# Twelve-stage decoder: latent attention's projections made pair by pair in two banks, and two expert mixtures reordered

## The chip, the cores and the metric

One core of a Trainium2 chip runs the whole program. The engines are TensorE (PE, with its weight loads PEld), VectorE (DVE), ScalarE (ACT), GpSimd (POOL) and SyncE (SP), which issues DMAs here. The metric is the device time of one execution in microseconds, median of the runs; lower is better.

## The reference

A decoder of four layers, each with an attention, a cross attention and a feed-forward part; after each of the twelve, x = layernorm(x + part(x)). x is 8 batches of 256 tokens, 256 wide, all in float32. The change touches four of the twelve parts:

```
_L0_xattn, _L1_xattn (latent attention, 16 heads of 64, context of 77 rows a batch):
    xn = layernorm(context); latn = layernorm(x); q = latn @ Wq
    k, v = split(concat([xn, latn]) @ Wkv)          # 77 + 256 = 333 keys
    out = softmax(q k' / 8) v @ Wo
_L0_ffn (mixture with silu, 8 experts, 2 chosen):
    probs = softmax(x @ router_w); topw, topi = top_k(probs, 2)
    routed = sum over the chosen e: topw * (silu(x @ w1[e]) @ w2[e])
    shared = sigmoid(x @ shared_gate_w) * ((silu(gate) * up) @ shared_down),  gate, up = x @ shared_gate_up
_L1_ffn (mixture with relu, 16 experts of 64, 4 chosen):
    sum over the chosen e: sel_val * (relu(x @ keys[e]) @ values[e])
```

## The kernel before

The twelve parts are twelve stages, `build[k](k)`, each with a program for every engine. Within one the engines meet at semaphores, each engine runs its instructions strictly in the written order, and nothing of one stage runs beside the next. x lives in SBUF by token (`x_nat`) and transposed (`x_t`). Two arenas of weights take turns: a stage's pack lies in one, the next pack is loaded into the other. PSUM is eight banks: `S.R` (2 x 2), `S.T` (2), `S.O` (2).

**Latent attention, `perceiver`** (stages 1 and 4). A prologue makes what batch 0 needs: `FIRST` lists its jobs. `lat` transposes the normalised latents, `q0` to `q3` project queries (four heads each), `c0` to `c4` transpose the contexts (only in the first such stage), `w0` to `w9` make the context values of all batches, which go to DRAM and come back by batch, `k0` to `k7` project the keys of one pair of heads each, `v0` to `v3` the values of half the heads for one block of keys. Then the loop over 8 batches of 8 pairs of heads. A pair on TensorE is: scores of both halves of the queries, the product of the pair before with its values, job slot 0, transposes of the first half, slot 1, transposes of the second half, slot 2. VectorE takes the maxima, copies the product, divides, and copies half of the transposes; ScalarE takes exponentials and copies the other half. `PERCEIVER_JOBS` names the jobs of the 24 slots of a batch: in the kernel before those of the next batch, but `o0`, `o1` (output projection) and `tail` (transposes of the new x), which belong to the batch before, and `v3`. All use one bank, `S_x`, so a job waits until the one before is copied out (`x_done`, counted over both copying engines). VectorE copies k and o, ScalarE all others.

**Silu mixture, `moe_silu`** (stage 2). TensorE makes the router's logits; VectorE ranks the choices and lays out 39 tiles of 128 rows, each with one expert. The shared expert runs for batches 0 to 4 beside that (`EARLY`), with the products and adds on POOL, for 5 to 7 behind the tiles. The tile loop: POOL issues an indirect gather (8 ahead, `XB`), TensorE transposes the rows, multiplies, transposes, multiplies, with copies on ScalarE and VectorE; POOL issues an indirect scatter into `planes` in DRAM, one plane for first and one for second choices. In the end both planes are read back by SP in four quarters, and x + weight 1 * plane 0 + weight 2 * plane 1 is built by VectorE, ScalarE (`weighed`) and POOL (`joined`), then normalised and transposed.

**Relu mixture, `moe_relu`** (stage 5). Four hidden units of two 128-wide blocks each for every batch; VectorE takes relu and gate in one step (`clipped`) out of PSUM; `outputs` multiplies by the values. The set-up of the gates is a VectorE chain; TensorE runs the hidden units of batch 0 and fillers (`keep_warm`, matmuls whose result nobody reads) beside it.

## Time and profile before

| | us |
|---|---|
| median of 3 runs | 3190.68 |
| lowest and highest run | 3190.6 and 3209.84 |
| the profiled execution's own time | 3193.03 |
| its span, first to last instruction | 3191.2 |
| TensorE busy in the span | 2893.4 (91%) |
| VectorE, ScalarE, POOL busy | 1909.2 (60%), 1192.7 (37%), 344.1 (11%) |
| mean granted TensorE clock | 0.97 |

Busy time of TensorE is modelled for the ends of matmuls. The stages that are touched lie at 376.8 to 978 (first perceiver), 978 to 1174 (silu mixture), 1336.8 to 1936.8 (second perceiver) and 1936.8 to 2090.9 (relu mixture). Names of tiles in the rows: `arena` is a pack of weights or a buffer in the spare arena, so `arena`, `v`, `k_t`, `q_t` alternate by batch.

### The profile page before, as it was taken

How to read it: one execution, taken by the hardware profiler on the slowest of the kernel's cores; microseconds unless marked ns; L12 is line 12 of the kernel's file. 1: busy time of each engine (PE TensorE's matmuls, PEld its weight loads, DVE VectorE, ACT ScalarE, POOL GpSimd, SP SyncE). 2: the span in 40 equal slices, each digit the busy share in tenths (PEclk: the TensorE clock that was granted, in tenths of full speed). 3: DMA queues.
4: the chain of work that ended last, by engine and by line, in shares of the span. 5: the costliest groups of instructions: out<-in, count | busy, mean ns of one | idle time of the engine just before them, and what ended most of it. 6: DMA issues, size and time to landing. Idle time of an engine off the chain costs nothing. (4 is left out here: it accounts for less than half of the span.)

```text
span 3191.2 us, 54962 instructions
## 1 busy us (share of the span) xinstructions
PE 2893.4 (91%) x22402; PEld 1838.4 (58%) x22402; DVE 1909.2 (60%) x3405; ACT 1192.7 (37%) x2549; POOL 344.1 (11%) x474
## 2 busy tenths in 40 slices
PE   6999899999988968799999989989999899989898
PEld 3565556666656746556666656856655433336576
DVE  4666347766774344447766773325547899985532
ACT  1332234444442333234444441123323476643111
POOL 1111100000003720000000000000011100000222
PEclk9999999999999979899999999989999999999899
DMA  3001010000011331010000000010000100000242
...
DMA packets 43419, 103.90 MB, mean 33 GB/s; under 512 B 4962, under 2 KB 32848, under 8 KB 39586
## 3 DMA queue, kind: packets, MB, share of 16 engines
...
## 5 line engine op out<-in xcount | busy, mean ns | idle before, releaser
L2360 ACT ACTIVATE prob<-R,neg_max 128x333 f32<-128x333 f32 x512 | 268.4, 537 | 209.1 <-DVE neg_max L2427 209.1
L3910 DVE TENSOR_TENSOR_SCAN arena<-arena,u 128x512 f32<-128x512 f32 x256 | 289.4, 1197 | 0.1
L2249 PE MATMUL T<-const,prob 128*128 128x128 f32 (+1 forms) x1536 | 211.4, 274 | 36.5 <-DVE prob L2440 23.4
L2249 PEld LDWEIGHTS T<-const,prob 128*128 128x128 f32 (+1 forms) x1536 | 181.2, 143 | 106.3 <-DVE prob L2440 68.6
L2440 DVE TENSOR_TENSOR prob<-prob,rec 128x666 f32<-128x666 f32 x256 | 218.3, 853 | 20.1 <-issue 1.3
L2427 DVE TENSOR_REDUCE neg_max<-R 128x2 f32<-128x666 f32 x256 | 205.3, 843 | 36.7 <-PE R L2238 36.7
L2367 ACT ACTIVATE prob_t<-T 128x384 f32<-128x384 f32 x256 | 125.5, 490 | 245.6 <-PE T L2249 239.3
L2433 DVE COPY prob_t<-T 128x384 f32<-128x384 f32 x256 | 141.9, 554 | 95.9 <-PE T L2249 80.8
L3841 ACT ACTIVATE arena<-delta,neg_a 128x510 f32<-128x510 f32 x256 | 176.0, 714 | 45.2 <-DVE arena L3910 44.3
L2186 PE MATMUL O<-keys_in,arena 128*128 128x333 f32 x512 | 174.6, 466 | 4.7 <-ACT attn_t L2342 1.4
L3744 PE MATMUL R<-arena,diag 64*64 64x512 f32 x1024 | 135.1, 616 | 26.5 <-DVE arena L3910 26.4
L2191 PE MATMUL O<-arena,keys_in 128*128 128x512 f32 x256 | 126.4, 617 | 2.6 <-ACT arena L2339 1.4
L2182 PE MATMUL O<-keys_in,arena 128*128 128x256 f32 x512 | 125.7, 389 | 2.4 <-ACT keys_in L2333 2.4
L2186 PEld LDWEIGHTS O<-keys_in,arena 128*128 128x128 f32 x512 | 87.9, 189 | 55.4 <-DVE arena L2408 5.4
L2209 PE MATMUL O<-arena,attn_t 128*128 128x256 f32 x512 | 118.9, 385 | 1.0 <-DVE ysb L2410 1.0
L944 DVE TENSOR_REDUCE neg_max<-R 128x8 f32<-128x2048 f32 (+1 forms) x24 | 55.0, 2291 | 100.0 <-PE R L721 100.0
L2209 PEld LDWEIGHTS O<-arena,attn_t 128*128 128x128 f32 x512 | 94.8, 190 | 25.2 <-issue 11.8
L2182 PEld LDWEIGHTS O<-keys_in,arena 128*128 128x128 f32 x512 | 92.1, 189 | 26.5 <-issue 10.8
L2360 ACT ACTIVATION_READ_ACCUMULATOR prob<-R,neg_max 128x1 f32 x512 | 103.9, 203 | 0.0
L2266 PE MATMUL O<-prob_t,v 128*64 128x256 f32 (+1 forms) x768 | 97.2, 388 | 1.3 <-DVE prob_t L2433 1.3
L2408 DVE COPY arena<-O 128x333 f32<-128x333 f32 x64 | 32.3, 504 | 109.1 <-PE O L2186 109.1
L2266 PE MATMUL O<-prob_t,arena 128*64 128x256 f32 (+1 forms) x768 | 97.2, 388 | 0.0
...
## 6 DMA issues: line engine op xcount, KB each, us to landing
...
```

The costliest lines, as they stand in the source:

```text
L2182: last = nc.tensor.matmul(bank[:, h * T:(h + 1) * T], wq[:, c, (2 * i + h) * P:(2 * i + h + 1) * P], keys[:, c, CTX:XK], start=(c == 0), s ...
L2186: last = nc.tensor.matmul(bank[:, 0:XK], wkv[:, c, i * P:(i + 1) * P], keys[:, c, :], start=(c == 0), stop=(c == C - 1))
L2209: last = nc.tensor.matmul(bank[:, 0:D], attn_t[:, b % 2, c, i * P:(i + 1) * P], wo[:, c, :], start=(c == 0), stop=(c == HP - 1))
L2249: last = nc.tensor.transpose(S.T[0:n, i, kc * P:(kc + 1) * P], prob[:, g % 2, i, first:first + n], S.ident)
L2266: last = nc.tensor.matmul(S_o[XD * i:XD * (i + 1), 0:T], v[b % 2][0:n, kc, (2 * hp + i) * XD:(2 * hp + i + 1) * XD], prob_t[0:n, m % 2, i, ...
L2360: last = nc.scalar.activation(prob[:, g % 2, i, :], S.R[:, g % 2, i * BANK:i * BANK + XK], ACT.Exp, bias=neg_max[:, g % 2, i:i + 1], accum ...
L2427: nc.vector.tensor_reduce(neg_max[:, g % 2, :], S.R[:, g % 2, :].rearrange("p (i n) -> p i n", i=2)[:, :, 0:XK], AX.X, ALU.max, negate=Tru ...
L2433: nc.vector.tensor_copy(prob_t[:, m % 2, 0, :, qt * P:(qt + 1) * P], S.T[:, 0, 0:3 * P].rearrange("p (c q) -> p c q", c=3)).then_inc(M.pt_ ...
L2440: nc.vector.tensor_tensor(prob[:, g % 2, :, :], prob[:, g % 2, :, :], rec[:, g % 2, :].unsqueeze(2).to_broadcast([P, 2, XK]), ALU.mult)\
L3744: last = nc.tensor.matmul(sums(i, a)[to:to + HB, :], diag[rows, i % CT, n + a, :], state[rows, (q + a) % HELD, :], start=(a == 1 and n == ...
L3841: nc.scalar.activation(decay[:, q % DEEP, :].rearrange("p (b t) -> p b t", b=PAIR)[:, :, 1:T], delta[:, i % 2, :].rearrange("p (b t) -> p ...
L3910: nc.vector.tensor_tensor_scan(state[:, q % HELD, :], decay[:, q % DEEP, :], u[:, i % 2, :], 0.0, ALU.mult, ALU.add)\
```

## The change

- `perceiver`: `FIRST` keeps `lat`, `q0`, the contexts, `v0` and `k0`. The other projections of a batch are made in its own loop, just ahead of the pair that needs them; `AHEAD` (`lat`, `v0`, `q0`, `k0`) still belong to the next batch. Slot 1 uses the bank of the products, `S_o`, slots 0 and 2 use `S_x`. Each bank's reuse waits for its own last job (`bank_free`), with a semaphore for each copying engine (`xa_done`, `xd_done`). The scores of a pair wait for its k and q. In the second perceiver the w jobs go first, and no fillers stand ahead of `lat` and `w0`. Statistics and normalisation of the next latents move.
- `moe_silu`: the shared expert's product and add go from POOL to VectorE, in alternating banks; its batches 5 and 6 go into the tile loop (`GATE_AT`, `UP_AT`, `OUT_AT`), 7 stays behind. The tiles use one bank for each step in place of two by turns. Six result buffers (`YB`) in place of four. In the end TensorE adds x (identity) and the second choices (diagonal matrices of their weights, made by ScalarE in the tile loop) in all eight PSUM banks, and VectorE adds the first choices out of SBUF.
- `moe_relu`: nine hidden units (`RAW`) are made ahead in place of four and the fillers; ScalarE takes their relu, VectorE multiplies by the gate later; `hid` has three buffers.

```diff
-PERCEIVER_JOBS = ("v3", "lat", None, "o0", "q0", None, "o1", "q1", None, "q2", "k0", "k1", "q3", "k2", "tail",
-                  "v0", "k3", "k4", "v1", "k5", "k6", "v2", "k7", None)
+PERCEIVER_JOBS = ("v2", "k1", None, "q1", "k2", "o0", "o1", "k3", None, "q2", "k4", "v1", "v3", "k5", "tail",
+                  "q3", "k6", "lat", "v0", "k7", None, "q0", "k0", None)
+AHEAD = ("lat", "v0", "q0", "k0")
 
 
 def perceiver(nc, S, k, contexts):
@@ -2094,21 +2095,27 @@
     def jobs(b, hp):
 
         for name in PERCEIVER_JOBS[3 * hp:3 * hp + 3]:
-            of = None if name is None else b - 1 if name[0] in "ot" else b if name == "v3" else b + 1
+            of = None if name is None else b - 1 if name[0] in "ot" else b + 1 if name in AHEAD else b
             yield (name, of) if of is not None and 0 <= of < B else None
 
-    FIRST = ("lat", "q0", "q1", "q2", "q3") + (("c0", "c1", "c2", "c3", "c4") if contexts else ()) + (
-        "w0", "w1", "w2", "w3", "w4", "w5", "w6", "w7", "w8", "w9",
-        "k0", "k1", "k2", "k3", "k4", "k5", "k6", "k7", "v0", "v1", "v2")
+    CONTEXTS = (("c0", "c1", "c2", "c3", "c4") if contexts else ()) + ("w0", "w1", "w2", "w3", "w4", "w5", "w6", "w7", "w8", "w9")
+    FIRST = (("lat", "q0") + CONTEXTS if contexts else CONTEXTS + ("lat", "q0")) + ("v0", "k0")
...
+            in_bank = [None, None]
+
+            def bank_free(slot):
+                if in_bank[slot % 2] is not None:
+                    name, of = in_bank[slot % 2]
+                    if name[0] in ACT_JOBS:
+                        pe.wait_ge(M.xa_done, acts_until(of, name))
+                    else:
+                        pe.wait_ge(M.xd_done, dves_until(of, name))
+
...
-                if (b, hp, slot) in job_at:
+                if (b, hp, slot) in steady:
                     name, of = list(jobs(b, hp))[slot]
-                    n = job_at[b, hp, slot]
-                    if n >= 1:
-                        pe.wait_ge(M.x_done, n)
-                    job(name, of, S_x)
+                    if slot == 1:
+                        if b + hp >= 1:
+                            pe.wait_ge(M.attn_ready, min(b * HP + hp, B * HP))
+                        bank_free(slot)
+                        job(name, of, S_o)
+                    else:
+                        bank_free(slot)
+                        job(name, of, S_x)
+                    in_bank[slot % 2] = (name, of)
...
-                if u == 0:
-                    if b == 0:
-                        pe.wait_ge(M.first_done, len(FIRST))
-                    else:
-                        pe.wait_ge(M.x_done, jobs_until(b - 1, "k7"))
+                if g == 0:
+                    pe.wait_ge(M.first_done, len(FIRST))
+                elif qt == 0 and (b >= 1 or hp >= 1):
+                    pe.wait_ge(M.xd_done, dves_until(b, f"k{hp}"))
+                    if hp % 2 == 0:
+                        pe.wait_ge(M.xa_done, acts_until(b, f"q{hp // 2}"))
...
+                bank_free(1)
                 if hp == 0:
                     pe.wait_ge(M.v_sb, 16 * (b + 1))
-                    if b >= 1:
-                        pe.wait_ge(M.x_done, jobs_until(b - 1, "v2"))
+                    pe.wait_ge(M.xa_done, acts_until(b, "v2"))
                 if hp == HP // 2:
-                    pe.wait_ge(M.x_done, jobs_until(b, "v3"))
+                    pe.wait_ge(M.xa_done, acts_until(b, "v3"))
...
-                if name in ("lat", "w0"):
+                if contexts and name in ("lat", "w0"):
                     keep_warm(nc, S, S.R[:, 0, 0:BANK], 4 if name == "lat" else 2)
-                if name in ("q0", "w0", "k0", "k1", "v0", "v1"):
+                if name == "q0" or name == "w0" and n:
                     pe.wait_ge(M.first_done, n)
                 elif n >= 2:
                     pe.wait_ge(M.first_done, n - 1)
...
                 beside(b, hp, 2)
                 if hp == 3 and b >= 1:
                     normalised(b - 1)
-                if hp == 4 and b + 2 < B:
-                    latent_statistics(b + 2)
-                if hp == 5 and b + 2 < B:
-                    latents(b + 2)
-            for hp in (1, 2):
+                if hp == 3 and b + 1 < B:
+                    latent_statistics(b + 1)
+                if hp == 4 and b + 1 < B:
+                    latents(b + 1)
+            for hp in range(1, HP):
                 for slot in range(3):
                     beside(B, hp, slot)
-            normalised(B - 1)
+                if hp == 3:
+                    normalised(B - 1)
             if contexts:
                 settle(dve, M.c_in, 16 * len(LC))
                 settle(dve, M.c_rstd, 1)
...
-    XB, YB = 8, 4
+    XB, YB = 8, 6
...
+    GATE_AT, UP_AT, OUT_AT = {8: 5, 20: 6}, {11: 5, 23: 6}, {15: 5, 27: 6}
...
+    scaled = spare[:, used:used + NT * D].rearrange("p (t d) -> p t d", t=NT)
+    weight = spare[:, used + NT * D:used + NT * (D + P)].rearrange("p (t n) -> p t n", t=NT)
     with ExitStack() as ctx:
...
+        def shared_bank(b, up):
+            return S.R[:, b % 2 if b < EARLY else 1, up * BANK:(up + 1) * BANK]
 
...
             sh_up(1)
-            sh_out(0)
             pe.wait_ge(G.picked, 1)
             pe.wait_ge(S.o_free[0], 1)
             flat = pick[:].rearrange("p j t e -> p (j t e)")
             nc.tensor.matmul(S.O[:, 0, 0:J * E], ones, flat, start=True, stop=True)
             nc.tensor.matmul(S.O[:, 1, 0:J * E], tri, flat, start=True, stop=True).then_inc(G.counted, 1)
-            sh_gate(2)
-            sh_up(2)
+            sh_out(0)
             sh_out(1)
-            sh_gate(3)
-            sh_up(3)
+            for b in (2, 3):
+                sh_gate(b)
+                sh_up(b)
             sh_out(2)
             to_table(0)
             to_table(1)
...
                     hidden_turned(i - 2)
                 if i >= 3:
                     product(i - 3, w_of.pop(i - 3))
+                if i in GATE_AT:
+                    sh_gate(GATE_AT[i])
+                if i in UP_AT:
+                    sh_up(UP_AT[i])
+                if i in OUT_AT:
+                    sh_out(OUT_AT[i])
...
+            def residual(b):
+                pe.wait_ge(G.sh_added, b + 1)
+                nc.tensor.matmul(banks[b], S.ident, S.x_nat[:, b * TT:(b + 1) * TT, :].rearrange("p t d -> p (t d)"),
+                                 start=True, stop=False, skip_group_check=True)
+
+            def second_choices(q):
+                pe.wait_ge(second_in[q], 16)
+                for tt in range(4 * q, 4 * q + 4):
+                    last = nc.tensor.matmul(banks[tt // TT][:, tt % TT * D:(tt % TT + 1) * D], weight[:, tt, :], plane[:, 1, tt, :],
+                                            start=False, stop=True, skip_group_check=True)
+                last.then_inc(G.summed, 1)
+
...
                                                    S.x_nat[:, b * TT + tt, c * P:(c + 1) * P], S.ident)
                 last.then_inc(G.xt_new, 1)
+
+            sh_gate(B - 1)
+            sh_up(B - 1)
+            pe.wait_ge(G.weights_made, NT)
+            for b in range(4):
+                residual(b)
+            sh_out(B - 1)
+            second_choices(0)
+            residual(4)
+            pe.wait_ge(G.sh_gate_sb, B)
+            residual(5)
+            second_choices(1)
+            residual(6)
+            second_choices(2)
+            turned(0)
+            turned(1)
+            residual(7)
+            second_choices(3)
+            for b in range(2, B):
+                turned(b)
             pe.sem_inc(G.past_all, 1)
 
...
             dve.drain().then_inc(G.picked, 1)
 
+            def sh_prod(b):
+                dve.wait_ge(G.sh_gate_sb, b + 1)
+                dve.wait_ge(G.sh_up_full, b + 1)
+                if b >= 2:
+                    dve.wait_ge(G.sh_out_full, b - 1)
+                nc.vector.tensor_tensor(prod[:, b % 2, :], sg[:, b % 2, :], shared_bank(b, 1), ALU.mult).then_inc(G.sh_prod, 1)
+
+            def sh_add(b):
+                dve.wait_ge(G.sh_scaled, b + 1)
+                x = S.x_nat[:, b * TT:(b + 1) * TT, :]
+                nc.vector.tensor_tensor(x, x, scaled[:, b * TT:(b + 1) * TT, :], ALU.add).then_inc(G.sh_added, 1)
+
+            sh_prod(0)
+            sh_prod(1)
             dve.wait_ge(G.counted, 1)
             nc.vector.tensor_copy(count[:], S.O[:, 0, 0:J * E].rearrange("p (c e) -> p e c", c=J))
             dve.drain()
@@ -3037,22 +3093,16 @@
             nc.vector.tensor_scalar(at_value[:, :, 0, :], at_tile[:], row_from_1[:], None, ALU.mult)
             nc.vector.tensor_tensor(at_value[:, :, 1, :], at_tile[:], order[:].unsqueeze(2).to_broadcast([P, J, NS]), ALU.mult)
             for i in range(4):
+                if i % 2 == 0:
+                    sh_prod(2 + i // 2)
                 some = slice(i * J // 4, (i + 1) * J // 4)
...
             nc.vector.tensor_scalar(holds[:], second[:], -1.0, 0.0, ALU.add, ALU.max)
             dve.drain().then_inc(G.rows_known, 1)
+            sh_prod(4)
+            nc.vector.tensor_tensor(behind[:], steps[:, 0:NS].unsqueeze(2).to_broadcast([P, NS, E]),
+                                    tile_end[:].unsqueeze(1).to_broadcast([P, NS, E]), ALU.is_gt)
+            dve.drain()
+            nc.vector.tensor_reduce(expert_f[:], behind[:], AX.X, ALU.add)
+            dve.drain()
+            nc.vector.tensor_scalar(expert_f[:], expert_f[:], float(E - 1), float(C * D), ALU.min, ALU.mult)
+            dve.drain()
+            nc.vector.tensor_copy(expert_at[:], expert_f[:])
+            dve.drain().then_inc(G.experts_known, 1)
+            dve.wait_ge(G.x_rows, 16)
 
             for i in range(NS + 1):
                 if i < NS:
                     dve.wait_ge(G.ht_full, i + 1)
                     if i >= 2:
                         dve.wait_ge(G.out_full, i - 1)
-                    nc.vector.tensor_copy(hid_t[:, i % 2, :, :], S.R[:, i % 2, BANK:BANK + FC * P].rearrange("p (f n) -> p f n", f=FC))\
+                    nc.vector.tensor_copy(hid_t[:, i % 2, :, :], S.R[:, 0, BANK:BANK + FC * P].rearrange("p (f n) -> p f n", f=FC))\
...
+                if i + 2 in UP_AT:
+                    sh_prod(UP_AT[i + 2])
+                if 2 <= i < 2 + EARLY:
+                    sh_add(i - 2)
+                if i in OUT_AT:
+                    sh_add(OUT_AT[i])
...
+            def sums(q):
+                dve.wait_ge(first_in[q], 16)
+                dve.wait_ge(G.summed, q + 1)
+                for tt in range(4 * q, 4 * q + 4):
+                    nc.vector.scalar_tensor_tensor(plane[:, 0, tt, :], plane[:, 0, tt, :], top[:, tt, 0:1],
+                                                   banks[tt // TT][:, tt % TT * D:(tt % TT + 1) * D], ALU.mult, ALU.add)
                 dve.drain()
                 for tt in range(4 * q, 4 * q + 4):
                     nc.vector.bn_stats(bst[:, tt, :], plane[:, 0, tt, :])
...
             neg_half = part(S.const, CONST, "neg_half")
 
-            def sh_prod(b):
-                pool.wait_ge(G.sh_gate_sb, b + 1)
-                pool.wait_ge(G.sh_up_sb, b + 1)
-                if b > 0:
-                    pool.wait_ge(G.sh_out_full, b)
-                nc.gpsimd.tensor_tensor(prod[:], sg[:], up[:], ALU.mult).then_inc(G.sh_prod, 1)
-
-            def sh_add(b):
-                pool.wait_ge(G.sh_scaled, b + 1)
-                x = S.x_nat[:, b * TT:(b + 1) * TT, :]
-                nc.gpsimd.tensor_tensor(x, x, scaled[:], ALU.add).then_inc(G.sh_added, 1)
-
...
-            sh_prod(0)
-            sh_prod(1)
             pool.wait_ge(G.x_rows, 16)
-            sh_add(0)
-            for b in range(2, EARLY):
-                sh_prod(b)
-                sh_add(b - 1)
             pool.wait_ge(G.rows_known, 1)
             for t in range(XB):
                 gather(t)
-            sh_add(EARLY - 1)
             for t in range(NS):
                 if t + XB < NS:
                     pool.wait_ge(G.xt_full, t + 1)
...
-            def joined(q):
-                pool.wait_ge(G.weighed, q + 1)
-                pool.wait_ge(G.sh_added, 2 * q + 2)
-                x = S.x_nat[:, 4 * q + 2:4 * q + 4, :]
-                nc.gpsimd.tensor_tensor(x, x, plane[:, 1, 4 * q + 2:4 * q + 4, :], ALU.add).then_inc(G.joined, 1)
-
...
                 if b >= 1:
-                    pe.wait_ge(M.exp_done, G * (b - 1) + g + 1)
+                    pe.wait_ge(M.raw_sb if n <= RAW else M.exp_done, n)
...
-            for g in range(1, G):
-                hidden(0, g)
-            keep_warm(nc, S, S.T[:, 1, :], 11)
+            for n in range(1, RAW):
+                hidden(n // G, n % G)
             settle(pe, M.setup, 1)
...
                     for g in range(G):
-                        if i >= 1:
+                        if i >= 1 and G * i + g >= RAW and i != RAW // G:
                             hidden(i, g)
                         if g == 1:
                             spread(i, 1)
+                if i == 0:
+                    for n in range(RAW, G * (RAW // G + 1)):
+                        hidden(n // G, n % G)
...
+            for n in range(RAW):
+                act.wait_ge(M.s_full, n + 1)
+                b, g = n // G, n % G
+                nc.scalar.activation(hid[:, b, 2 * g:2 * g + 2, :].rearrange("p c t -> p (c t)"), hidden_bank(g), ACT.Relu).then_inc(M.raw_sb, 1)
...
             def clipped(b, g):
+                some = hid[:, b % 3, 2 * g:2 * g + 2, :].rearrange("p c t -> p (c t)")
+                if G * b + g < RAW:
+                    dve.wait_ge(M.raw_sb, G * b + g + 1)
+                    dve.wait_ge(M.kg_ready, 2 * b + g // 2 + 1)
+                    nc.vector.tensor_tensor(some, some, gates[:, g // 2, g % 2, :], ALU.mult).then_inc(M.exp_done, 1)
+                    return
                 dve.wait_ge(M.s_full, G * b + g + 1)
                 dve.wait_ge(M.kg_ready, 2 * b + g // 2 + 1)
```

## Rows read from the trace of the kernel before

**Rows 1.** Busy time by window: perceiver's start and batches 0, 4 and 7 of it; silu; second start.

```profile
core 0: us, PE busy (x) PEld busy (x) DVE busy (x) ACT busy (x) POOL busy (x), PEclk, DMA share, GB/s
376.79:430.41 53.62, 47.23 (x142) 24.97 (x143) 11.31 (x37) 15.10 (x28) 3.34 (x6) 1.00 0.20 71
430.41:493.35 62.94, 58.35 (x328) 36.29 (x328) 44.40 (x84) 31.00 (x91) 0.93 (x2) 1.00 0.00 1
561.11:628.87 67.76, 67.59 (x377) 43.72 (x377) 47.71 (x94) 32.19 (x93) 1.87 (x4) 1.00 0.02 6
899.90:952.07 52.17, 40.43 (x266) 26.53 (x265) 37.21 (x71) 23.32 (x72) 0.93 (x2) 1.00 0.24 97
...
1021.06:1121.60 100.54, 91.87 (x471) 74.05 (x471) 32.99 (x78) 30.73 (x80) 77.04 (x78) 0.97 0.31 94
1121.60:1173.03 51.43, 27.42 (x104) 21.98 (x104) 23.83 (x73) 18.00 (x35) 11.59 (x14) 0.71 0.25 82
1336.84:1388.39 51.55, 45.59 (x132) 24.01 (x132) 7.44 (x21) 13.55 (x23) 1.85 (x4) 1.00 0.17 62
```

**Rows 2.** Busy time by window: pairs with jobs o q, q k k, v k, and none.

```profile
567.99:577.58 9.59, 9.59 (x58) 7.30 (x57) 5.75 (x11) 4.25 (x13) 0.00 (x0) 1.00 0.00 0
587.17:595.92 8.75, 8.72 (x49) 5.69 (x48) 6.06 (x11) 4.30 (x13) 0.00 (x0) 1.00 0.00 0
621.45:628.87 7.42, 7.42 (x41) 4.17 (x41) 5.41 (x10) 3.27 (x10) 0.00 (x0) 1.00 0.01 3
924.70:931.42 6.72, 4.50 (x34) 2.76 (x33) 4.96 (x9) 3.17 (x10) 0.00 (x0) 1.00 0.00 1
```

**Rows 3.** Timeline, TensorE: inside pair 587.17:595.92, and the scores behind 621.45:628.87.

```profile
589.93 2.00 PE L2182 MATMUL O<-keys_in,arena 128*128 128x256 f32 x8
591.77 0.82 PE L2249 MATMUL T<-const,prob 128*128 128x128 f32 x6
592.62 1.39 PE L2186 MATMUL O<-keys_in,arena 128*128 128x333 f32 x4
593.84 0.82 PE L2249 MATMUL T<-const,prob 128*128 128x128 f32 x6
...
628.87 0.30 PEld L2238 LDWEIGHTS R<-k_t,q_t 64*128 64x128 f32 x4 [0.17 <-DVE k_t L2408]
```

**Rows 4.** Timeline, start of the first perceiver, around the contexts.

```profile
384.60 1.70 DVE L2489 TENSOR_SCALAR arena<-arena,cmv,crs 128x256 f32<-128x256 f32 x5 [0.75 <-POOL crs L2554]
...
388.88 0.35 PEld L2205 LDWEIGHTS O<-const,arena 128*128 128x128 f32 x2
...
394.56 17.41 PE L2199 MATMUL O<-arena 128*128 128x512 f32 x40 [1.29 <-ACT keys_in L2321]
...
416.62 0.29 SPq L2163 DMA_DIRECT2D arena<-context_values  x1
```

**Rows 5.** Timeline, start of the second perceiver, ScalarE ahead of the w jobs.

```profile
1350.02 1.69 ACT L2377 ACTIVATE arena<-ctx_hat,arena 128x616 f32<-128x616 f32 x2
1351.61 0.78 ACT L2321 ACTIVATE keys_in<-ctx_hat,arena 128x77 f32<-128x77 f32 x2
```

**Rows 6.** Silu mixture: POOL's adds by line (ns min/median/max), then its timeline.

```profile
L3142 POOL TENSOR_TENSOR x_nat<-x_nat,scaled x5: 1266/1272/2473, 993.8 to 1031.1; 128x512 f32<-128x512 f32 x5
...
1015.93 0.18 DVE L3063 TENSOR_SCALAR holds<-second 128x39 uint32<-128x39 f32 x1
...
1033.87 1.03 PE L2833 MATMUL O<-arena,hid_t 128*128 x4
...
1036.04 1.03 PE L2833 MATMUL O<-arena,hid_t 128*128 x4
...
1125.33 8.89 SPq L2715 DMA_DIRECT2D arena<-planes  x8
...
1134.23 0.88 DVE L3104 SCALAR_TENSOR_TENSOR arena<-arena,top 128x256 f32<-128x256 f32 x2
...
1135.19 1.40 DVE L3107 BATCH_NORM_STATS2 bst<-arena 128x6 f32<-128x256 f32 x4
```

**Rows 7.** Timeline, relu mixture: TensorE's fillers under the set-up of the gates.

```profile
1946.14 9.60 PE L212 MATMUL T<-ctx_t,const 128*128 128x512 f32 x22
```

257 lines of the change are left out of this document (98 added, 159 removed).

## The prediction

> **What bounds the kernel now.** The granted clock comes first: it is 0.97 over the span, so TensorE nearly always runs at the higher of its two levels, 2.4 GHz. Then the strip of busy tenths: TensorE is at nine tenths or more nearly everywhere. What is to be found are the places where it has nothing to do, and those that it fills with work that could lie in a hole. So I cut the span at the stages that the change touches and read busy time by window [rows 1]. In a middle batch of a perceiver TensorE is busy 67.59 of 67.76 us: bound by TensorE. In its last batch it is busy 40.43 of 52.17 us: no jobs are left, and the chain scores, maximum, exponential, share, transposition sets the time. The 53.62 and 51.55 us ahead of the first scores are serial work that nothing covers. In the silu mixture the tile loop lasts 100.54 us with 78 indirect DMAs on POOL, 1.29 us for each, and TensorE at 91.87; its end lasts 51.43 us with TensorE at 27.42 and a clock of 0.71.
>
> Within a perceiver I read single pairs of heads [rows 2] and the order inside one [rows 3]. A pair without jobs takes 6.72 us and TensorE is busy 4.50: that is the floor. The costs are from start to start: scores and product together 2.76 (587.17 to 589.93), a q job 1.84, a k job 1.22. A transposition takes 0.85 in front of k, where it also waits for the bank; its six matmuls without a wait I estimate at 0.70, and 0.76 in front of the scores. TensorE's base is then 2.77 + 0.70 + 0.76 = 4.23. An o job is then 9.59 - 4.23 - 1.83 = 3.53; I use 3.56. The check: q, k, k gives 4.23 + 1.83 + 2.44 = 8.50, and 8.75 was measured. v, k gives 7.28, measured 7.42. So 0.14 to 0.25 us of a pair is waiting, mostly for the single bank S_x.
>
> **The change, part by part.**
>
> *First perceiver, start.* q1 to q3, k1 to k7, v1 and v2 leave the prologue. Not all of it shortens. Without the three q jobs, the context transposes can start only when VectorE's normalisation ends at 384.60 + 1.70 = 386.3 [rows 4], where they began at 388.88; so about 2.5 us of the q jobs' 5.2 is gained. The ten w jobs start 2.5 us earlier, at 392.1, and take 17.2. v0 follows at once, since it no longer waits for the last copy: 392.1 + 17.2 + 1.7 (v0) + 1.2 (k0) + 0.75 (copy) = 413.0, against 430.41: **-17.4**. The values that the first product needs are written by five DMAs behind the w jobs and were read back from 416.62 on, which becomes 414.1. The first product comes about a pair after the first scores, at 421, so a read of up to 7 us stays covered; beyond that each us is lost once.
>
> *Second perceiver, start.* Without contexts, w0 to w9 now go first. ScalarE's three steps, which stood behind the q copies [rows 5], start with the stage: 1337.0 + 1.69 + 0.78 = 1339.5 for w0, + 17.2 = 1356.7. Then lat, whose statistics ran meanwhile: 1.9 with its copy; q0 1.75, v0 1.7, k0 1.2 and its copy 0.75 end at 1364.1. The scores began at 1388.39: **-24.3**. The bounds are -22 and -25.
>
> *Middle batches.* The same 20 jobs, in two banks by turns. What goes is the bank wait: 8 x 4.23 + 8 x 1.83 + 2 x 3.56 + 8 x 1.22 + 2 x 0.6 = 66.56 against 67.76, -1.2 a batch, six batches: **-7.2** for each perceiver. The bounds: 0 (something else waits in its place) and -9. What is late next is the copy of the pair's own k. The k job lies in slot 1 of the pair before, and the scores wait for VectorE's copy. The pair that already ends so took 7.42 us, and its scores started 0.17 us after that copy let them [rows 2, 3]. Behind that wait on TensorE's queue stand the product and all jobs, and the maxima wait for the scores; I take nothing for it, since the copy ends together with the second transposition. The moved layer norm steps (statistics and latents of the next batch, now after pairs 3 and 4) lie on VectorE under v1 and tail, and the two context steps on ScalarE under the scores.
>
> *First and last batch.* Batch 0 takes on v2, k1 to k7, q1 to q3 and v1, but hands lat, q0, v0 and k0 of batch 1 over as before: 66.56 less two o and tail is 58.8, plus 2.0 for two pairs on the floor = 60.8, against 62.94 [rows 1]: -2.1. In batch 7 its own jobs fill the hole. Seven pairs: 7.28, 10.84, 9.01, 9.11, 7.88, 7.28, 6.8 = 58.2, against 52.17: +6.0. So each perceiver's loop changes by -2.1 - 7.2 + 6.0 = **-3.3**, both by -6.6. The hole is where the gain of the starts comes from: 12 jobs of 18 us leave a stretch in which TensorE was the path, and come back where it had 12 us idle.
>
> *Silu mixture.* POOL loses the shared products and adds (five of each, the adds 1.27 us in the median), and gathers at once when the rows are known. They were known at 1016.11 [rows 6], and the first gather came at 1021.06. VectorE's chain to that point gains 1 us (counts ahead of sh_out(0)) and about 3 where it ran beside POOL, and takes on four products of 0.7: known at about 1013.5, first gather -7.5. In the loop POOL alone would end 7.5 us earlier. But TensorE, at 2.17 us a tile [rows 6], takes on the shared parts of 5 and 6: six jobs of 1.8 us. 1016.5 + 41 x 2.17 + 10.8 + 0.9 = 1117.2, against 1121.60: **-4.4**. The planes' DMA starts 3.7 us after the loop [rows 6], then 3.3. In the end VectorE gives the pace. For a quarter: four sums 1.84, statistics 1.47, the rest 0.8, together 4.1 us; before, it stood behind ScalarE, POOL and products. The planes' first quarter lands 5.6 us after 1120.5; adding the second choices on TensorE 1.7; four quarters 16.6; root, normalise, transpose, copy 5.4: 1150 against 1173.03: **-23** with the loop's 4.4 inside it. Bounds -14 and -27: the first if the loop gains nothing and the quarters take as much longer as TensorE needs at the low clock, the second if TensorE's extra jobs fit into its waits.
>
> Beside the loop VectorE now adds x and the shared part, eight times 0.7 us. One add of POOL took 2.47 us, where the median is 1.27 [rows 6], and VectorE was at work then. The Trainium skill (SBUF — State Buffer, Who interferes with whom) says that a VectorE instruction with two SBUF inputs contends with a GpSimd instruction that reads SBUF, and that the second to issue waits for the whole first. By that rule the change also takes stretched instructions away ahead of the loop, which the row agrees with; inside the loop it would delay POOL by at most 8 x 0.7 = 5.6 us, which leads to the first rival.
>
> *Relu mixture.* Five hidden units of 1.73 us (8 matmuls of the q job's form) leave the loop and stand where 22 filler matmuls took 9.60 us under the gate's set-up [rows 7]. ScalarE's nine relu steps lie in its empty time. VectorE multiplies as before. **-8.5**; bounds -6 and -9.5.
>
> *Clock.* No filler stands ahead of the second perceiver's w0, so TensorE pauses 2.7 us or more there, and 2.5 us in the first where the q jobs were. The granted clock fell to 0.71 in the end of the silu mixture, where TensorE had long pauses [rows 1]. Low for some 4 us costs 2: **+2**, from 0 to +5.
>
> The sum: -17.4 - 24.3 - 6.6 - 23 - 8.5 + 2 = **-77.8 us**. It is made against a profiled execution of 3193.03 us (span 3191.2 and 1.8 around it), 0.07% over the median of 3190.68. The same difference from the median gives 3112.9; I say 3113. Beyond 1% a difference is more than this kernel's measurement may confuse with none.
>
> **The rivals.**
> 1. The silu mixture gives a third. For it: TensorE and POOL are both near full in the loop, POOL would be held up by VectorE's adds, and TensorE works at the low clock in the end, where it now gets more to do. Against it: the end's 51 us are a chain through four engines, each busy less than 28 us, that the change cuts to one. It gives 8 in place of 23: 3128.
> 2. The hole does not take the jobs: in the last batch each pair is lengthened by its jobs in full, and so by 12 jobs of 18 us in place of what I count. That is +12 for each perceiver: 3137. For it: a pair's jobs could lie after its chain and not beside it. Against it: the middle pairs run jobs and chain side by side, 8.75 us where the two alone would be 6.72 + 4.27.
> 3. A wait takes the bank wait's place, and this is the way to slower: the scores wait in each of 128 pairs for the copy of their k (on VectorE) or q (on ScalarE), made just before. At 0.25 us a pair, +32: 3145. It decides at 78 / 128 = 0.61 us a pair; at 0.9, the kernel is at 3228. For it: VectorE and ScalarE carry copies and chain in a fixed order, and nothing is made early any more. Against it: the one pair in eight that is built so showed 0.17.
> 4. The change does not do what it says: prologue jobs leave, but the first scores come no earlier, since the context values' round trip through DRAM sets the first product. It would hold the loops back by the about 10 us between the present product and the read: 3133.
>
> **How the numbers follow.** Forecast, 3098 to 3126: 0.66. Rival 1: 0.12. Rival 2: 0.06. Rival 3: 0.10, of which 0.03 slower by over 1% and 0.02 within it. Rival 4: 0.06. The predicted time is the first's. The range for 8 in 10 takes in rival 1, rivals 2 and 4 in part, and the deep ends of silu, loops and relu: 3094 to 3136. Faster by over 1% (under 3158.8): 0.94; within 1%: 0.03; slower: 0.03.
>
> **What would show it.** The first scores of the perceivers 17 and 24 us sooner against their stages' starts; a middle batch at 66.6 us, with k's copy and the scores less than 0.2 us apart; a last batch that takes 58 us to its last pair's scores; the first gather some 7 us sooner against the silu mixture's start; the end of that mixture in about 33 us, with VectorE as its chain; no fillers ahead of relu's gates. I would be wrong if pairs grew by waits on k or q, if the silu loop got longer than 100 us, or if the clock in the second prologue stood at the lower level for most of it.

## The result, and the profile after

The changed kernel takes 3099.22 us (median of 4 runs, 3095.31 to 3103.52), the kernel before 3190.64 (4 runs, 3186.81 to 3209.84). The ratio is 0.9702, with a 95% interval of 0.9661 to 0.9743. The profiled execution's span is 3093.5 us, against 3191.2; it is the fastest of its four, and the one before lies a little over its median, so the spans differ by more than the medians (97.7 and 91.4 us).

First the windows of the changed kernel that answer to [rows 1] (us, busy us of each engine with its instructions, granted clock, DMA share, GB/s). In order: start, batches 0, 4 and 7, and end of the first perceiver; tile loop and end of the silu mixture; start of the second perceiver.

```profile
core 0: us, PE busy (x) PEld busy (x) DVE busy (x) ACT busy (x) POOL busy (x), PEclk, DMA share, GB/s
370.65:407.06 36.41, 31.37 (x82) 14.35 (x82) 6.26 (x24) 12.22 (x23) 2.36 (x4) 0.95 0.24 87
407.06:465.67 58.61, 56.29 (x328) 36.32 (x328) 44.67 (x84) 31.14 (x91) 0.95 (x2) 1.00 0.04 12
660.85:725.91 65.06, 65.00 (x378) 43.50 (x377) 47.99 (x94) 32.28 (x93) 1.87 (x4) 1.00 0.02 6
856.20:913.53 57.33, 55.74 (x325) 37.32 (x324) 40.91 (x78) 26.33 (x77) 0.93 (x2) 1.00 0.22 88
913.53:943.12 29.59, 25.30 (x101) 14.90 (x101) 8.64 (x19) 4.26 (x12) 0.93 (x2) 0.88 0.00 1
...
977.21:1080.56 103.35, 100.13 (x534) 84.98 (x534) 40.15 (x92) 37.44 (x103) 78.83 (x78) 1.00 0.30 91
1080.56:1119.40 38.84, 24.66 (x96) 16.96 (x95) 16.11 (x58) 14.04 (x27) 4.78 (x10) 0.84 0.33 108
...
1281.90:1310.55 28.65, 24.20 (x60) 11.45 (x61) 2.36 (x8) 10.46 (x18) 0.93 (x2) 0.94 0.27 100
```

The hole of the last batch is filled: TensorE is busy 55.74 of 57.33 us, where it was busy 40.43 of 52.17 [rows 1]. A middle batch takes 65.06 us in place of 67.76 and is still all TensorE. Set against the terms of the prediction, each read between the same marks in both traces (VectorE's first instruction of the stage, first scores, last pair's scores, the next stage's first matmul; the silu loop from the first to the last indirect DMA, which sets its end 2.04 us later in the trace before than the window in [rows 1]):

| term | predicted | measured |
|---|---|---|
| perceiver 1, start | -17.4 | 53.52 to 36.32: -17.2 |
| perceiver 2, start | -24.3 | 51.48 to 28.42: -23.1 |
| batch 0, each | -2.1 | -4.3 and -4.1 |
| six middle batches, each perceiver | -7.2 | -16.0 and -16.2 |
| last batch, each | +6.0 | +5.2 |
| perceivers' ends | 0 | +2.8 (clock 0.88) and +0.1 |
| silu mixture | -23 | 195.71 to 176.30: -19.4 |
| relu mixture | -8.5 | 154.09 to 146.46: -7.6 |
| clock, not in the other terms | +2 | in the starts and ends |
| the eight stages that the diff doesn't touch | 0 | -3.1 |
| sum | -77.8 | -97.7 |

The untouched stages differ singly by -6.1, +0.3, -6.6, +7.5, -1.7, +1.9, +1.5 and +0.1 us, with the granted clock going both ways (0.93 to 0.97 in one, 0.99 to 0.93 in the next). Such differences are between executions: over the fourteen traces of this case the first stage, the same code in all, takes 368.6 to 377.3 us. Of the 20 us by which the sum missed, 18 stand in one term, the middle batches; the others nearly cancel. Windows of single pairs (q, k, o; o, k; v, k with lat's copies; q, k; and k alone), which answer to [rows 2]:

```profile
667.98:678.56 10.58, 10.58 (x61) 7.91 (x60) 6.06 (x11) 4.26 (x12) 0.00 (x0) 1.00 0.00 1
678.56:687.67 9.11, 9.04 (x53) 6.43 (x52) 6.68 (x15) 2.68 (x9) 0.93 (x2) 1.00 0.01 2
711.63:718.76 7.13, 7.13 (x41) 4.23 (x40) 5.18 (x10) 5.03 (x15) 0.00 (x0) 1.00 0.00 0
718.76:725.91 7.15, 7.15 (x46) 4.99 (x45) 5.51 (x10) 3.77 (x11) 0.00 (x0) 1.00 0.00 0
906.57:913.53 6.96, 5.43 (x37) 3.47 (x36) 5.47 (x10) 3.17 (x10) 0.00 (x0) 1.00 0.00 0
```

And the timeline inside the pair 718.76:725.91 (start, length, engine, line, operation), which answers to [rows 3]:

```profile
721.53 2.00 PE L2191 MATMUL O<-keys_in,arena 128*128 128x256 f32 x8
...
723.37 0.82 PE L2276 MATMUL T<-const,prob 128*128 128x128 f32 x6
...
724.02 1.29 PE L2195 MATMUL O<-keys_in,arena 128*128 128x333 f32 x4
...
725.14 0.82 PE L2276 MATMUL T<-const,prob 128*128 128x128 f32 x6
...
725.35 0.51 DVE L2436 COPY k_t<-O 128x333 f32<-128x333 f32 x1 [0.57 <-PE O L2195]
...
725.91 1.39 PE L2265 MATMUL R<-k_t,q_t 64*128 64x333 f32 x8
```

From start to start: q 1.84, transposition 0.65, k 1.12, transposition 0.77. I had priced k at 1.22 and the transposition ahead of it at 0.70. The k copy ends at 725.86 and the scores start at 725.91, behind a transposition that runs to 725.96, 0.77 us after its start, as long as from 923.93 to 924.70 in the trace before, where no k was waited for: the wait on k costs nothing in a full pair. In the last batch's pair with k alone it costs nothing either. That pair takes 6.96 us, with 6.72 for a pair without jobs before [rows 2], and the 0.24 us lie between its two transpositions, where the k job now stands in place of the wait for the copy of the first. TensorE has so much time there that a job of 1.12 us costs 0.24.

### The profile page after: what moved, and what is told of

It is laid out like the page before. It is cut to its first block and busy times, and to the rows that moved or that the text cites. A ratio compares the mean times of both kernels' runs of the same rounds, so it can differ in the third digit from the quotient of the medians.

```text
span 3093.5 us, 55363 instructions
## 1 busy us (share of the span) xinstructions
PE 2841.6 (92%) x22416; PEld 1831.1 (59%) x22416; DVE 1909.1 (62%) x3404; ACT 1199.2 (39%) x2567; POOL 326.5 (11%) x460
## 5 line engine op out<-in xcount | busy, mean ns | idle before, releaser
L2195 PE MATMUL O<-keys_in,arena 128*128 128x333 f32 x512 | 164.8, 444 | 0.0
L3770 PEld LDWEIGHTS R<-arena,diag 64*64 64x64 f32 x1024 | 29.3, 133 | 112.9 <-DVE arena L3936 78.6
## 6 DMA issues: line engine op xcount, KB each, us to landing
arena<-pack_dram SPq DMA_DIRECT2D x2, 4100.0 KB, 15.2
```

The source lines that it names most:

```text
L2195: last = nc.tensor.matmul(bank[:, 0:XK], wkv[:, c, i * P:(i + 1) * P], keys[:, c, :], start=(c == 0), stop=(c == C - 1))
L3770: last = nc.tensor.matmul(sums(i, a)[to:to + HB, :], diag[rows, i % CT, n + a, :], state[rows, (q + a) % HELD, :], start=(a == 1 and n == ...
```

## The experiments

The runs were made on three chips. The kernel before took 3217.63 us on the first, 3213.54 on the second, 3192.31 on the third, so ratios to it are compared, and times of stages from the traces. No run takes the relu mixture alone; its gain is read from its stage, which takes 154.1 to 155.4 us in the four traces with the old code and 144.8 to 148.1 in the ten with the new.

**One bank again.** In slot 1 the job goes back to the bank of slots 0 and 2, everything else as changed:

```
-                    if slot == 1:
-                        if b + hp >= 1:
-                            pe.wait_ge(M.attn_ready, min(b * HP + hp, B * HP))
-                        bank_free(slot)
-                        job(name, of, S_o)
...
+                    bank_free(0)
+                    job(name, of, S_x)
+                    in_bank[0] = (name, of)
```

> The changed kernel, but slot 1 uses the bank S_x again, in both perceivers; the order of the jobs is the new one. Theory: a middle batch went from 67.76 to 65.06 us because the second bank takes away the bank wait, so here it is back at 67.2 to 67.8, in both perceivers, with batch 0 some 2 us longer than the 58.61 of the changed kernel and the last batch 0 to 2 us longer than 57.33: in all about +17 us for each perceiver, the kernel at about 3133. Rival: the new order (jobs of a batch just ahead of their pairs) saves the time, or the two copying engines being counted apart does; then a middle batch stays within 0.5 us of 65.06 and the kernel within 5 us of 3099.

Measured: 3160.82 us, ratio 0.9828 (0.9791 to 0.9864). The middle batch is at 67.88 us, just over the forecast's 67.8. The rival falls with it: the new order and the two copying engines counted apart are still there, and gain nothing by themselves. Batch 0 is at 60.75 and the last at 59.38, both 2.1 longer; the loop of each perceiver takes 527.4 us in place of 506.4, so it costs 21 and not 17 us. The wait itself stands on TensorE's weight loads ahead of k, for the copy of the q or v before it, and ahead of slot 2, for that of k:

```profile
910.79 0.86 PEld L2195 LDWEIGHTS O<-keys_in,arena 128*128 128x128 f32 x4 [0.26 <-ACT q_t L2358]
...
912.78 0.30 PEld L2202 LDWEIGHTS O<-arena,keys_in 128*128 128x128 f32 x2 [0.17 <-DVE k_t L2430]
```

Yet the window of such a batch shows TensorE busy 67.66 of 67.88 us:

```profile
674.09:741.97 67.88, 67.66 (x378) 43.83 (x377) 47.99 (x94) 32.31 (x93) 1.87 (x4) 1.00 0.02 6
```

The changed kernel's batch shows 65.00 us busy with the same 378 matmuls, so of the 2.8 us of waiting 2.7 are counted as work. The ends of matmuls are modelled, so such a row can't say what a wait costs: 67.59 of 67.76 us [rows 1] did not mean that only 0.17 us were to be had.

**Two banks, old order.** The kernel before with the second bank alone (and, as the change has it, a semaphore for each copying engine):

```
-                    n = job_at[b, hp, slot]
-                    if n >= 1:
-                        pe.wait_ge(M.x_done, n)
-                    job(name, of, S_x)
+                    if slot == 1 and b + hp >= 1:
+                        pe.wait_ge(M.attn_ready, min(b * HP + hp, B * HP))
+                    bank_free(slot)
+                    job(name, of, S_o if slot == 1 else S_x)
+                    in_bank[slot % 2] = (name, of)
```

> The kernel before with one thing of the change, in both perceivers: slot 1 uses the products' bank S_o, with a semaphore for each copying engine. The jobs, their order and the prologue are the old ones; silu and relu mixtures too. With one bank the new order gave 67.87 us for a middle batch, the old one 67.76, so theory: the banks alone make it 65.0 to 65.4 here, batch 0 loses some 2.5 us of its 62.94, the last batch (few jobs) at most 0.5 of 52.17, the starts nothing: both perceivers together -36 us, a ratio of 0.988 to 0.990. Rival: the two banks help only where q or v and k alternate by slot, as in the new order; in the old one o, q and k of a pair stand two slots apart in the same bank. Then a middle batch stays above 66 us and the ratio above 0.993.

Measured: 3180.42 us, ratio 0.9896 (0.9866 to 0.9927), middle batches of 65.23 us, starts unchanged at 53.52 and 51.46. A middle batch, the last one with its hole open as before, and a single pair:

```profile
681.15:746.38 65.23, 64.97 (x378) 43.50 (x377) 47.77 (x94) 32.18 (x93) 1.87 (x4) 1.00 0.02 6
876.85:930.60 53.75, 42.02 (x266) 27.17 (x265) 37.33 (x71) 23.42 (x72) 0.93 (x2) 0.97 0.23 94
706.95:715.20 8.25, 8.25 (x49) 5.63 (x48) 6.07 (x11) 4.31 (x13) 0.00 (x0) 1.00 0.00 0
```

The third window is the pair q, k, k of [rows 2], with nothing changed but the bank: 8.25 us in place of 8.75. The pair v, k went from 7.42 to 7.13. The last batch is 1.6 us longer than in the trace before and not 0.5 at most, but another trace of the old perceiver has 53.74 as well, so that isn't the bank's doing; a loop's time is known to some 1.5 us.

With the changed kernel, the one before and the run above, this splits the change of the perceiver (first perceiver, from the first scores to the last pair's):

| loop, us | one bank | two banks |
|---|---|---|
| old order, start 53.52 us | 521.66 | 506.45 |
| new order, start 36.3 us | 527.37 | 506.47 |

So the whole gain of the loop is the banks' (15.2 us), and the whole gain of the start is the order's. The order costs the loop nothing with two banks and 5.7 us with one: alone it would have kept 11.5 of its 17.2 us. Of the batches, 0 gets 2.5 us shorter against this run, five of the six middle ones 0.2 to 0.4, and the last 3.6 longer.

**k right ahead of its scores.** Slots 1 and 2 change places, so that nothing stands between k and the scores that need it:

```
-PERCEIVER_JOBS = ("v2", "k1", None, "q1", "k2", "o0", "o1", "k3", None, "q2", "k4", "v1", ...
+PERCEIVER_JOBS = ("v2", None, "k1", "q1", "o0", "k2", "o1", None, "k3", "q2", "v1", "k4", ...
```

> The changed kernel, but in each pair the k job of the next pair goes from slot 1 to slot 2, right ahead of the scores that need it, and what stood in slot 2 goes to slot 1. This gives the third rival of the prediction (the scores wait for a copy made just before) a wait that it surely has. k's copy ends about 0.75 us after its matmuls, and nothing of TensorE stands between: each pair grows by 0.6 to 0.8 us, a middle batch from 65.06 to 70 to 71.5 us, the two perceivers together by 75 to 95 us, and the kernel is at 3175 to 3195, about the 3190 of the kernel before: the point of 0.61 us a pair from which that rival decides. If VectorE's copy is hidden in another way (the product's bank, a shorter wait on transposes), a batch stays under 67 us and the kernel under 3130.

Measured: 3286.38 us, ratio 1.0218 (1.0171 to 1.0264): slower than the kernel before. A middle batch takes 75.19 us, 10.1 more and not 5 to 6.5. The forecast of the copy was right, and something else came on top. A pair with tail in slot 1, on TensorE and VectorE:

```profile
752.12 0.87 PE L2276 MATMUL T<-const,prob 128*128 128x128 f32 x6
...
753.69 0.85 PE L2276 MATMUL T<-const,prob 128*128 128x128 f32 x6 [0.26 <-DVE prob_t L2461]
...
754.37 1.29 PE L2195 MATMUL O<-keys_in,arena 128*128 128x333 f32 x4
...
755.70 0.51 DVE L2436 COPY arena<-O 128x333 f32<-128x333 f32 x1 [0.57 <-PE O L2195]
...
756.26 1.39 PE L2265 MATMUL R<-arena 64*128 64x333 f32 x8 [0.60 <-DVE arena L2436]
```

The last row shows the price that I asked for, 0.60 us of waiting for k. The second shows what k did in slot 1: it stood between the two transpositions, which share the bank T, and covered the copy of the first. Where slot 1 now holds o or v, which cover that copy as well, a pair is 0.66 us longer (11.25 against 10.59, 9.51 against 8.85); with tail or lat there, 1.1 to 1.3; where it is empty, 1.54 to 1.79 (8.67 against 7.13, 10.90 against 9.11). So of the 10.1 us a batch some 5.3 are the wait for k, as forecast, and 4.8 the copy that nothing covers. The third rival's mechanism is real: at 0.66 us in 128 pairs, 84 us, the wait alone would have taken nearly the whole gain (an estimate from these pairs). The kernel is free of it because each k has a transposition behind it.

**Perceivers alone, silu mixture alone.** The kernel before with one function of the changed kernel each.

> The kernel before with the whole change of the perceiver alone; silu and relu mixtures are the old ones. By the stages of the changed kernel's trace: 29.6 and 37.9 us less, together 67.5, a ratio of 0.979, with middle batches of 65.06 us, first scores 36.4 and 28.5 us behind their stages' starts. Were the stages not independent (the clock, weights still loading), the ratio would be off by more than 0.002.

> The kernel before with the change of the silu mixture alone. By the stage's length in the two traces, 195.7 and 176.3 us: -19.4 us, a ratio of 0.994 (on whichever chip). First gather 34 us behind the stage's start, tile loop some 3 us longer than before, end from the loop on 39 us in place of 53. If the shorter stage came from what the changed perceiver ahead of it leaves (TensorE's clock at its start), it would be under -12 us, a ratio over 0.996.

Measured: 3145.98 us, ratio 0.9784 (0.9763 to 0.9806), and 3193.99 us, ratio 0.9937 (0.9915 to 0.9959). By these two the perceivers' change is worth 2.2% and the silu mixture's 0.6%, as the stages say, and with the relu mixture's 7.6 us they give 0.970, so the parts add up; first scores come 35.87 and 28.82 us behind the starts. On that chip, though, the silu mixture itself takes 217.3 and 218.0 us with the old code and 203.0 with the new. The tile loop is what differs: 122.5 and 125.4 us in the two kernels with the old code there, 129.1 in the one with the new, against 102.6 and 103.4 in the first two traces. The loop of this last kernel (its trace is of the slowest of eight executions, 3186.59 to 3209.65 us), and one of its scatters:

```profile
1012.91:1142.04 129.13, 110.23 (x534) 87.40 (x535) 39.21 (x92) 37.05 (x103) 77.62 (x78) 0.96 0.24 73
...
1027.34 1.02 POOL L3164 DMA_INDIRECT planes<-ye,dest  x1 [3.19 <-DVE ye L3115]
```

POOL's 78 DMAs take as long as ever (77.62 us busy), but twelve times it stands for 1.2 to 3.2 us, 30.2 us in all, until VectorE has copied a result; in the changed kernel's first trace no such wait is over 1 us. What makes ScalarE's and VectorE's copies late the trace doesn't name. The old loop is nearly as much longer, so it isn't of the change; what it is stays open. The forecast for the loop, 3 us longer, can't be judged on that chip.

**POOL's pause in the end of the silu mixture.** From the last indirect DMA to the next stage the end took 38.86 us; the prediction's steps put it at some 32 between these marks. In the changed kernel (POOL, ScalarE, TensorE, VectorE):

```profile
1093.61 1.04 POOL L3195 TENSOR_TENSOR rstd<-mv,const 128x4 f32<-128x4 f32 x1 [13.04 <-DVEq L3163]
1101.18 0.20 POOL L3197 TENSOR_TENSOR shift<-mv,rstd 128x4 f32<-128x4 f32 x1 [6.54 <-issue]
...
1101.41 2.07 ACT L2986 ACTIVATE x_nat<-arena,shift,rstd 128x256 f32<-128x256 f32 x4 [13.15 <-POOL shift L3197]
...
1102.56 2.10 PE L2901 MATMUL O<-const,x_nat 128*128 128x128 f32 x8 [7.41 <-ACT x_nat L2986]
...
1107.32 1.03 PE L2893 MATMUL T<-arena 128*128 128x256 f32 x4
...
1108.45 0.87 DVE L3152 SCALAR_TENSOR_TENSOR arena<-arena,top,R 128x256 f32<-128x256 f32 x2 [6.78 <-PE T L2893]
```

POOL stands 6.54 us between its first root and the product behind it, for nothing that the profile shows. The normalisation waits for that, TensorE's first transposes wait for the normalisation, the last second choices stand behind them on its queue, and VectorE, the engine that sets the pace, waits 6.78 us. The trace of the kernel before has the same 6.54 us ahead of the same product, although POOL had run five products of the shared expert in that stage, the last just ahead of the indirect DMAs, and two adds behind them:

```profile
1018.39 1.26 POOL L3137 TENSOR_TENSOR prod<-sg,up 128x512 f32<-128x512 f32 x1 [10.75 <-PE T L2761]
...
1139.83 1.26 POOL L3172 TENSOR_TENSOR x_nat<-x_nat,arena 128x512 f32<-128x512 f32 x1 [6.59 <-ACT arena L2933]
1141.05 1.04 POOL L3177 TENSOR_TENSOR rstd<-mv,const 128x4 f32<-128x4 f32 x1
1148.63 0.21 POOL L3179 TENSOR_TENSOR shift<-mv,rstd 128x4 f32<-128x4 f32 x1 [6.54 <-issue]
```

Two ways out, first to run root and product once on spare columns while POOL is idle, then to move the transposes:

```
             pool.sem_inc(G.past_tiles, 1)
+            nc.gpsimd.tensor_tensor(rstd[:, 12:16], top[:, 12:16, 0], neg_half[:, 0:4], ALU.pow)
+            pool.drain()
+            nc.gpsimd.tensor_tensor(shift[:, 12:16], top[:, 12:16, 0], rstd[:, 12:16], ALU.mult)
+            pool.drain()
```

> The changed kernel, but behind the tile loop of the silu mixture POOL runs one root and one product on four other columns (each written again by the real ones), in time in which it is idle. In the end of that mixture POOL stood still for 6.54 us between the first root and the first shift, with no releaser, in the kernel before and in the changed one alike; ScalarE's normalisation, TensorE's first transposes and, queued behind them, the last second choices waited for it. Theory: a cost of the first such instructions on POOL. Then the pause moves ahead of the first statistics (1093.6 us) and the end from the tile loop on gets 4 to 7 us shorter than its 38.86 us. Rival: the pause belongs to what happens then (the read of the planes under way), and stands between first real root and shift again; the end stays within 1 us of 38.86.

```
             second_choices(2)
-            turned(0)
-            turned(1)
             residual(7)
             second_choices(3)
-            for b in range(2, B):
+            for b in range(B):
```

> The changed kernel, but on TensorE's queue in the end of the silu mixture the transposes of batches 0 and 1 go behind the last x and the last second choices. Theory: VectorE's 6.8 us of idle time ahead of the last quarter's sums come from that order, since the transposes wait for a normalisation that waits for POOL. Then the last quarter's sums start about 6 us sooner, right behind the third quarter's, but the end gains less, 2 to 4 us of 38.86, since ScalarE's 13 us of normalisations and copies start at the same time as before and now set it. Rival: POOL's pause alone is the limit, the end stays within 1 us of 38.86.

Measured: ratio 0.9691 (0.9656 to 0.9726), end 32.31 us, 6.6 shorter; and ratio 0.9702 (0.967 to 0.9735), end 37.70 us, 1.2 shorter. With root and product early the pause has moved with them:

```profile
1110.95 1.08 POOL L3191 TENSOR_TENSOR rstd<-top,const 128x4 f32<-128x4 f32 x1
1118.57 0.20 POOL L3193 TENSOR_TENSOR shift<-top,rstd 128x4 f32<-128x4 f32 x1 [6.54 <-issue]
1124.05 1.01 POOL L3199 TENSOR_TENSOR rstd<-mv,const 128x4 f32<-128x4 f32 x1 [5.28 <-DVEq L3163]
1125.20 0.20 POOL L3201 TENSOR_TENSOR shift<-mv,rstd 128x4 f32<-128x4 f32 x1
```

With the transposes last, the last quarter's sums start 21.3 us behind the loop in place of 27.9, and the end hardly gains: ScalarE's chain still starts behind POOL's pause. That is less than the 2 to 4 us that I expected: the queue's order carried the wait to VectorE, but the pause was the cause, and it holds up ScalarE as well. Then the product alone, without a root ahead of it:

```
+            nc.gpsimd.tensor_tensor(shift[:, 12:16], top[:, 12:16, 0], top[:, 12:16, 1], ALU.mult)
+            pool.drain()
```

> The changed kernel, but behind the tile loop POOL runs one product alone on four columns (no root ahead of it). In the run with root and product early the pause of 6.54 us stood between those two, 13 us ahead of where it had been. Theory A: it belongs to the first product on POOL in this stage; then it stands ahead of the early product or is short there, and none stands behind the first real root: the end is 32 to 33 us. Theory B: it belongs to what follows a first root (its drain or its code); then it stands again between the first real root and the shift, and the end stays at 38 to 39.5 us. Ratio 0.9675 by A, 0.970 by B.

Measured: 3094.32 us, ratio 0.9693 (0.9673 to 0.9712), end 32.26 us. There is no pause any more, at no place:

```profile
1080.98 0.22 POOL L3191 TENSOR_TENSOR shift<-top 128x4 f32<-128x4 f32 x1
1094.00 1.04 POOL L3197 TENSOR_TENSOR rstd<-mv,const 128x4 f32<-128x4 f32 x1 [12.80 <-DVEq L3163]
1095.19 0.20 POOL L3199 TENSOR_TENSOR shift<-mv,rstd 128x4 f32<-128x4 f32 x1
```

The end's time is theory A's, but A had allowed for the pause to show at the early product. The median doesn't show the gain: it is that of the changed kernel beside it, 3094.82 us, and the ratio is nearer to theory B's. Five us are at the edge of what five executions tell; the stage in the trace shows them, 171.28 us and not 176.42. What is shown: behind the 78 indirect DMAs the pause comes when POOL's first product follows a root, and not when a product stands ahead of that root. Products ahead of the DMAs don't prevent it, as the trace before shows, nor do adds behind them. Why is open. The Trainium skill (GPSIMD Engine Reference, 2.1 Instruction dispatch) says that the first call of newly loaded code on this engine costs about 6 us, with no instruction in the profile. The size and the look agree with 6.54 us, but no run shows that code was loaded, and that a product ahead of the root is free is not in that rule.

**Shared parts out of the loop.** Batches 5 and 6 of the shared expert behind the tile loop:

```
-    GATE_AT, UP_AT, OUT_AT = {8: 5, 20: 6}, {11: 5, 23: 6}, {15: 5, 27: 6}
+    GATE_AT, UP_AT, OUT_AT = {}, {}, {}
```

with their gates, products and adds in the same order ahead of those of batch 7.

> The changed kernel, but the shared expert's batches 5 and 6 stand behind the tile loop again and not in it (batches 0 to 4 are added by VectorE in the loop as before). The prediction took TensorE as the loop's bound, with 10.8 us of shared products in it, and kept as the first rival that TensorE and POOL, both near full, give little. If TensorE sets the loop, it gets 5 to 10 us shorter and the end 7 to 10 us longer: the mixture changes by less than 4 us. If POOL with its 78 DMAs of 1.3 us sets it (101.4 us of 103.35), the loop gains 2 us at most and the end loses 7 to 10: the mixture is 5 to 8 us longer, the ratio 0.972.

Measured: 3110.85 us, ratio 0.9731 (0.9706 to 0.9755). Loop and end in this kernel:

```profile
982.62:1085.31 102.69, 93.74 (x486) 74.77 (x487) 37.54 (x88) 35.23 (x97) 78.94 (x78) 1.00 0.30 92
1085.31:1134.92 49.61, 35.41 (x144) 26.32 (x143) 18.68 (x62) 16.92 (x33) 4.81 (x10) 0.84 0.27 85
```

Against the changed kernel on the same chip (loop 103.27, end 39.07) the loop gains 0.6 us and the end loses 10.5. POOL sets the loop where it takes 103 us: 78 DMAs, 78.9 us busy and 0.30 between them. TensorE's six shared jobs in it are free. No run takes apart the rest of the mixture's change (the earlier first gather, the sums in PSUM, the result buffers); these are read from the traces.

**The changed kernel again, and the best one.** On that chip too: the changed kernel itself, and one with root and product early and with two fillers ahead of the second perceiver's w0:

```
-                if contexts and name in ("lat", "w0"):
+                if contexts and name == "lat" or name == "w0":
```

> The changed kernel itself, so that the variants of this call have it on their own chip. Its ratio to the kernel before was 0.9702; the variants that touch only the silu mixture's end gave 0.9691 to 0.9702 on two other chips, on which the tile loop took 122 to 129 us with the old code and the new, in place of 103. Expected here: 0.969 to 0.971 on either kind of chip; first scores of the perceivers 36.3 and 28.4 to 30 us behind their stages' starts, middle batches of 65.06 us.

> The changed kernel with POOL's first root and product behind the tile loop of the silu mixture (as in the run that made its end 32.3 us), and two fillers again ahead of w0 in the second perceiver, under ScalarE's three context steps. The root gives 6 to 7 us. Fillers: if the pause of 4 us on TensorE ahead of w0 makes its clock fall (0.94 over that start of 28.65 us), the clock there goes to 1.00 and 1 to 2 us are won; if the fall comes from pauses in the stage ahead, nothing changes. Together 6 to 9 us under the changed kernel, a ratio of 0.967 to 0.968.

> The kernel with root and product early and with the two fillers ahead of the second w0, beside the changed kernel on the same chip. The end of the silu mixture at 32.3 us against 38.9 (6.6 us less), the second perceiver's first scores 27.6 us behind its start against 28.4 to 30. Together 7 to 9 us, a ratio 0.0025 under that of the changed kernel: 0.9675. If the 6.6 us were lost behind (clock, next stage), the ratio would be that of the changed kernel.

Measured: the changed kernel 3094.82 us, ratio 0.9678 (0.9659 to 0.9697); the other 3116.9 us, ratio 0.9701 (0.9675 to 0.9727) on the second chip, short of what was expected and with no changed kernel beside it, and 3085.01 us, ratio 0.9653 (0.9634 to 0.9672), on the third. Side by side it is 9.8 us faster, a little over the 7 to 9 expected, though the two intervals overlap. Of that, the silu mixture's stage shows 5.3 (176.42 to 171.08, its end 39.07 to 32.25) and the second perceiver's start 0.6; the rest isn't placed. The second perceiver's first scores come 27.64 and 27.75 us behind its start in the two runs with fillers, 28.37 and 28.42 in the changed kernel's two traces with the same granted clock of 0.94, and 28.8 to 30.0 in seven others at 0.88 or 0.89. That fillers win 0.7 us is so likely. That they keep the clock up is not shown: it was 0.94 in both runs with them, but in two of nine without them too.

## Why the prediction was right, and where it was not

It said 3113 us and -77.8; the medians say 3099.22 and -91.4, the two profiled executions -97.7. Direction, mechanism and range held, though the forecast's own 3098 to 3126 only just. By its steps:

- *Starts.* -17.4 and -24.3 against -17.2 and -23.1. Adding instructions along the path worked, down to the wait for VectorE's normalisation. The second start is 1.2 us longer than reckoned, at a granted clock of 0.94 where it had been 1.00; in seven other traces, at 0.88 or 0.89, it is 0.4 to 1.6 us longer still. The clock had a term of its own.
- *Middle batches: the step that failed in size.* "What goes is the bank wait", -1.2 a batch; it was -2.7. The mechanism is shown by the two runs that give and take the bank (67.88 and 65.23 us). The term was mis-sized in its prices. k at 1.22 was read from start to start in a kernel that waited for its bank, and held a piece of the wait: it is 1.12 with two banks and 1.23 with one, in the same order. The transposition in front of a job was an estimate of 0.70 and is 0.65, and lat and tail, put at 0.6, add 0.42. The three make up the 1.5 us between 66.56 and 65.06. The check against two measured pairs left 0.25 and 0.14 us as waiting; the bank gave back 0.51 and 0.29 in the same two pairs, twice as much. The bound of -9 for six batches was passed by far.
- *First and last batch.* -2.1 and +6.0 against -4.2 and +5.2, the first off mainly by the same prices. "The hole is where the gain of the starts comes from" is shown, and needs the second bank to be right in full: with it the new order costs the loop nothing, with one bank 5.7 us.
- *Silu mixture.* First gather -8.1 (predicted -7.5), and the end's chain is VectorE's, with 4.1 to 4.4 us for a quarter, reckoned at 4.1. Two steps failed, in opposite directions. TensorE was taken as the loop's bound with 10.8 us of new work; it came to the job behind the loop 7.4 us sooner than before and not 4.4, since POOL is the bound. And POOL's pause of 6.54 us, which the trace of before has, was left out of the "5.4 us" for root, normalisation, transpose and copy. That the mixture came within 4 us of its term is so in part luck. With the pause taken away the stage is 5 us shorter still, -24.6 in all. The sign "if the silu loop got longer than 100 us" was badly put: it was over that before, 100.54 [rows 1], and the sum itself had 103.6 for it (1013.6 to 1117.2). Between its first and last DMA it takes 103.35 us, 102.58 before.
- *VectorE's adds in the loop.* I allowed up to 5.6 us of hold-up for POOL. Its 78 DMAs took 78.8 us in place of 77.5, three of them 1.4 to 1.5 us where the longest had been 1.21. Each of the three was issued 0.06 to 0.14 us after one of the adds of 0.68 us had begun; four other adds in the loop began while an issue was under way, and neither add nor issue got longer. By the Trainium skill's rule (SBUF — State Buffer, Who interferes with whom) the second to issue would wait for the whole first. The trace agrees for the three where POOL was second, though it shows 0.4 to 0.5 us for each and not the rest of the add, and shows nothing of it for the four where VectorE was.
- *Relu mixture.* -7.6 against -8.5.
- *Clock.* +2 was about right, but it stood in other places too: 2.8 us in the first perceiver's end, at 0.88.
- *The rivals.* The first, silu gives a third: no, 84% of the forecast. The second, the hole does not take the jobs: no. The fourth, the context values' way through DRAM: no, the first pair takes 6.69 us (6.44 before). The third, the scores wait for k or q: not here. With k one slot later the kernel is 2.2% slower than before, at 1.3 us a pair against the 0.61 at which I had put the turning point, but half of that is the uncovered copy, which the rival didn't have. It was the right one to fear.
